# A fused four-layer graph network on one core: sums of squares by transposes and a VectorE sum, inverse degrees spread by two DMAs, incidence products earlier

## What is computed

```python
def hypergraph_conv(x, adj, W, b):
    H = (adj != 0).astype(x.dtype)
    w = adj.reshape(N, -1)[:, :C]            # first row of adj
    xw = jnp.einsum('ncd,hd->nch', x, W)
    Dn = jnp.einsum('nce,ne->nc', H, w)
    Dn = jnp.where(Dn > 0, 1.0 / Dn, 0.0)    # inverse degrees of the nodes
    Be = 1.0 / H.sum(axis=1)
    m = Be[:, :, None] * jnp.einsum('nce,nch->neh', H, xw)
    return Dn[:, :, None] * jnp.einsum('nce,neh->nch', H, m) + b
h = jax.nn.relu(hypergraph_conv(x, adj, W1, b1))      # 512 features
h = layer_norm(h, gamma, beta)                         # needs the mean of h*h
y = hypergraph_conv(h, adj, W2, b2)
```

## Time and profile before

| what | us |
|---|---|
| median of 3 runs | 1412.56 |
| lowest and highest of them | 1412.31, 1417.0 |
| span of the profiled execution | 1411.1 |
| PE busy | 1367.8 (97%) |
| DVE busy | 1271.7 (90%) |
| ACT busy | 1053.6 (75%) |
| POOL busy | 946.2 (67%) |

### The profile page before, as it was taken

How to read it: one execution, slowest core, us unless ns; L and a number is a source line. 1 busy time by engine, 2 the same in 40 slices (tenths; PEclk the granted TensorE clock), 3 DMA queues, 4 the chain that set the end, 5 groups by cost and what they waited for, 6 DMA issues and landing times.

```text
span 1411.1 us, 33599 instructions
## 1 busy us (share of the span) xinstructions
PE 1367.8 (97%) x8954; PEld 1249.5 (89%) x8954; DVE 1271.7 (90%) x5267; ACT 1053.6 (75%) x2345; POOL 946.2 (67%) x972
## 2 busy tenths in 40 slices
PE   7789999999999999999999999999999999999986
PEld 6678999999999999999999999999999999999975
DVE  6879999999999999999999999999999999999884
ACT  4557777877777887777887777787777788777764
POOL 5657766667766666766666776666786666676533
PEclk9899999999999999999999999999999999999999
DMA  4000111101111101111110111110111111111001
GB/s 127 31 31 23 39 39 54 54 23 45 52 39 50 52 29 43 47 52 37 52 47 27 45 52 37 52 52 22 45 52 45 44 52 35 39 45 37 31 31 53
DMA packets 75384, 62.16 MB, mean 44 GB/s; under 512 B 3013, under 2 KB 70985, under 8 KB 75338
## 3 DMA queue, kind: packets, MB, share of 16 engines
q1 hardware_dynamic: 75338, 61.63, 13.7%
HBM read 36.45 MB, written 16.78 MB: 38 GB/s over the span
## 4 chain that ended last, share of the span: by engine, by line
PE 92%; DVE 5%; issue 2%; ACT 1%; POOL 0%; DMA 0%; DVEq 0%; ACTq 0%; POOLq 0%
PE ps L371 39%; PE ps L356 25%; PE ps L375 20%; PE ps L477 4%; PE ps L432 3%; DVE stats L1590 1%; DVE prod L1774 1%; PE ps L633 0%; DVE h L1602 0%; DVE x L1737 0%; PE ps L629 0%; DVE x L1685 0%; DVE z L1730 0%; DMA adj_f<-in_adjT 0%; DVE el L1675 0%
## 5 line engine op out<-in xcount | busy, mean ns | idle before, releaser
L1315 POOL TENSOR_TENSOR x3n<-p,x 128x512 f32<-128x512 f32 x63 | 80.9, 1284 | 259.8 <-ACT p L982 259.8
L1275 POOL TENSOR_TENSOR hT_lo<-hT,hT_hi 128x512 fp32r<-128x512 f32 x126 | 161.3, 1302 | 57.0 <-ACT hT L924 42.1
L1255 POOL TENSOR_TENSOR rs<-var_e,neg_half 128x4 f32<-128x4 f32 x160 | 165.2, 1033 | 23.7
L903 ACT ACTIVATE p<-ps,rs 128x256 f32<-128x256 f32 (+1 forms) x256 | 136.6, 597 | 29.1 <-DVE sij L1691 28.8
L371 PE MATMUL ps<-wl_hi,h2T_hi 128*128 128x512 f32 (+1 forms) x512 | 149.1, 373 | 0.7 <-DVE x L1737 0.7
L356 PE MATMUL ps<-p,alT 128*128 128x256 f32 (+1 forms) x512 | 142.9, 382 | 0.5 <-DVE p L1715 0.5
L371 PE MATMUL ps<-wl_lo,h2T_hi 128*128 128x512 f32 (+1 forms) x512 | 132.8, 341 | 0.0
L375 PE MATMUL ps<-wl_hi,h2T_lo 128*128 128x512 f32 (+1 forms) x512 | 132.2, 340 | 0.0
L1590 DVE BATCH_NORM_STATS2 stats<-x 128x6 f32<-128x256 f32 x256 | 108.8, 425 | 5.7
L1000 ACT ACTIVATE h3T_hi<-ps 128x512 fp32r<-128x512 f32 x64 | 38.3, 598 | 91.0 <-PE ps L477 87.1
L924 ACT ACTIVATE hT_hi<-ps,cols_sb 128x512 fp32r<-128x512 f32 x128 | 87.4, 683 | 21.7 <-PE ps L375 21.5
(11 more groups left out here) (192 smaller groups left out, 4607.8 us busy)
## 6 DMA issues: line engine op xcount, KB each, us to landing
x_in<-in_x SPq DMA_DIRECT2D x32, 512.0 KB, 3.5
out_x<-x SPq DMA_DIRECT2D x32, 512.0 KB, 3.2
adj_f<-in_adjT SPq DMA_DIRECT2D x32, 256.0 KB, 2.8
adj_m<-in_adjT SPq DMA_DIRECT2D x32, 256.0 KB, 2.9
adj_l<-adj_m SPq DMA_DIRECT2D x32, 256.0 KB, 2.4
vqk<-in_l_wk SPq DMA_DIRECT2D x3, 256.0 KB, 4.6
x<-in_w1T SPq DMA_DIRECT2D x1, 512.0 KB, 6.7
x<-in_w2T SPq DMA_DIRECT2D x1, 512.0 KB, 7.7
```

Of the source, the lines that this page charges most:

```text
L903: return act.activation(dst, src, ACT.Copy, scale=scale)
L1255: pool.tensor_tensor(rs[:, layer, :], var_e[:, layer, :], neg_half[:], ALU.pow).then_inc(done, G)
L1275: pool.tensor_tensor(hTs[1][:, hc, :], hT[:, hc, :], hTs[0][:, hc, :], ALU.subtract).then_inc(S["hT_lo"], 1)
L1315: pool.tensor_tensor(x3n[:, s], p0[:, s], x2[:, s], ALU.add).then_inc(S["x3_ready"], 2)
```

## The change

It has three parts. First, `front_sums` no longer multiplies the squares with a column: it transposes each 128x128 block of `sq` into the banks `z` (columns 260 to 387), and DVE sums every row of it (`front_squares`, new, at the head of `front_variance`); the factor 1/512 moves into the last operation of the variance. Second, for all groups but the first two (`early`), the inverse degrees are spread by DMA: SP stores the column of four to a row in DRAM, waits for it, and loads that row into all 128 partitions (`spread_degrees`); `next_d` leaves PE's loop, and `next_gt` reads the SBUF tile `deg_sp` in place of the PSUM bank. Third, `next_s` moves on PE from between two `front_c2` to right behind `front_sums`, into the banks 7 and 5 in place of 3 and 4; `copy_s` on ACT and `next_degrees` on DVE move forward with it, and `copy_s` now copies the degrees too, so that DVE reads them from `s_sb`.

```diff
+        deg_row = nc.dram_tensor("deg_row", [1, G * C], F32, kind="Internal").ap()
+        deg_sp = sb("deg_sp", G, C)
+        s_sb = sb("s_sb", G, C + 1)
...
+        def early(r):
+            return not r.steady and r.i < 1
+        def s_bank(r):
+            return "s" if early(r) else "s2"
...
             def load_adj(r):
                 wait(sp, S["pen_ready"], r.front(G))
+                wait(sp, S["gt_ready"], r.front(G))
...
+            def spread_degrees(r):
+                sp.wait_ge(S["deg_ready"], r.next(G))
+                with nc.allow_non_contiguous_dma(reason="a column of four becomes a row"):
+                    sp.dma_start(deg_row.rearrange("a (g p) -> p (a g)", g=G), deg[:, 2, :]).then_inc(S["rd_stored"], 16)
+                sp.wait_ge(S["rd_stored"], r.loads(r.i - 1))
+                sp.dma_start(deg_sp[:].rearrange("p g c -> p (g c)"),
+                             deg_row.broadcast_to((P, G * C))).then_inc(S["rd_loaded"], 16)
...
             def next_s(r, b):
-                if b == 0:
-                    wait(pe, S["z_ready"], r.front(G))
+                if early(r):
+                    if b == 0:
+                        wait(pe, S["z_ready"], r.front(G))
+                elif b == 0:
+                    wait(pe, S["p2_copied"], r.mid(G))
                 elif b == 1:
-                    wait(pe, S["zb_ready"], r.mid(G))
+                    wait(pe, S["p2_copied"], r.mid(2))
...
             def late_h3(r, b):
                 if b == 0:
                     wait(pe, S["p2_copied"], r.mid(2))
+                    if r.has_next:
+                        wait(pe, S["s_copied"], r.next(G))
...
             def front_sums(r, g):
                 pe.wait_ge(S["sq_done"], r.front(G))
-                product(bank("z", g)[:, D + 2:D + 3], lambda c: sq[:, 0, g * C:(g + 1) * C],
-                        lambda c: mean_w[:, 0:1], 1).then_inc(S["hsums_ready"], 1)
+                pe.transpose(bank("z", g)[:, SQ:SQ + P], sq[:, 0, g * C:(g + 1) * C],
+                             ident[:]).then_inc(S["hsums_ready"], 1)
...
                     front_sums(r, 3)
+                if r.has_next:
+                    next_s(r, 0)
+                    next_s(r, 1)
                 if r.has_mid:
                     mid_b2(r)
...
                     mid_ap(r, 0)
-                if r.has_next:
-                    next_d(r)
...
             def degrees():
-                b = BANK["s"]
-                return (ps[:, b[0]:b[1] + 1:b[1] - b[0], 0:2 * (C + 1)]
-                        .rearrange("p b (g c) -> p b g c", g=2)[:, :, :, C])
+                return s_sb[:, :, C]
...
             def next_gt(r):
                 dve.wait_ge(S["s_copied"], r.next(G))
-                dve.wait_ge(S["rd_spread"], r.next(G))
-                dve.tensor_tensor(gt[:], bank("d").rearrange("p (g c) -> p g c", g=G), s_sb[:],
-                                  ALU.mult).then_inc(S["gt_ready"], G)
+                if early(r):
+                    dve.wait_ge(S["rd_spread"], r.next(G))
+                    rows_of = bank("d").rearrange("p (g c) -> p g c", g=G)
+                else:
+                    dve.wait_ge(S["rd_loaded"], r.loads(r.i - 1))
+                    rows_of = deg_sp[:]
+                dve.tensor_tensor(gt[:], rows_of, s_sb[:, :, 0:C], ALU.mult).then_inc(S["gt_ready"], G)
...
+            def front_squares(r):
+                dve.wait_ge(S["hsums_ready"], r.front(G))
+                dve.tensor_reduce(hsq[:], four("z")[:, :, SQ:SQ + P], AX_X, ALU.add).then_inc(S["hsq_ready"], G)
             def front_variance(r):
-                dve.wait_ge(S["hsums_ready"], r.front(G))
+                front_squares(r)
...
-                dve.tensor_tensor(hmean[:, 1, :], four("z")[:, :, D + 2], hmean[:, 0, :],
-                                  ALU.subtract).then_inc(S["hvar_ready"], G)
+                dve.wait_ge(S["hsq_ready"], r.front(G))
+                dve.scalar_tensor_tensor(hmean[:, 1, :], hsq[:], 1.0 / DH, hmean[:, 0, :], ALU.mult,
+                                         ALU.subtract).then_inc(S["hvar_ready"], G)
...
                     tail_norm(r)
+                if r.has_next:
+                    next_degrees(r)
                 if r.has_late:
                     late_low(r, 0)
```

More of the change, by code:

```diff
@@ L79, in gnn_stack @@
     K2, K1, K0, KALL = 0, D + 2, 2 * D + 2, 3 * D + 2
+    SQ = D + 4
     R = {}
@@ L146, in gnn_stack @@
         hmean = sb("hmean", 2, G)
+        hsq = sb("hsq", G)
         z = sb("z", G, D)
@@ L325, in body @@
                     load_mask(past)
+                if r.has_next:
+                    spread_degrees(r)
             def opening(r):
@@ L499, in mid_p10 @@
                     wait(pe, S["p2_copied"], r.mid(G))
+                    if r.has_next:
+                        wait(pe, S["s_copied"], r.next(2))
                 elif g == 2:
                     wait(pe, S["x1_ready"], r.front(2))
+                    if not r.steady and r.i == 1:
+                        wait(pe, S["s_copied"], r.next(G))
                     if not r.steady and r.i == GROUPS:
@@ L539, in front_sums @@
                 pe.wait_ge(S["sq_done"], r.front(G))
-                product(bank("z", g)[:, D + 2:D + 3], lambda c: sq[:, 0, g * C:(g + 1) * C],
-                        lambda c: mean_w[:, 0:1], 1).then_inc(S["hsums_ready"], 1)
+                pe.transpose(bank("z", g)[:, SQ:SQ + P], sq[:, 0, g * C:(g + 1) * C],
+                             ident[:]).then_inc(S["hsums_ready"], 1)
             def mid_ap(r, g):
                 if g == 0:
-                    if not r.steady and r.i == 1:
-                        wait(pe, S["deg_ready"], r.next(G))
+                    wait(pe, S["zb_ready"], r.mid(G))
                 elif g == 1:
@@ L695, in body @@
                     front_c2(r, 2)
-                if r.has_next:
-                    next_s(r, 0)
-                    next_s(r, 1)
-                if r.has_front:
                     front_c2(r, 3)
@@ L975, in copy_s @@
                 act.activation(s_sb[:, 2 * b:2 * b + 2, :],
-                               bank("s", b)[:, 0:2 * (C + 1)].rearrange("p (g c) -> p g c", g=2)[:, :, 0:C],
+                               bank(s_bank(r), b)[:, 0:2 * (C + 1)].rearrange("p (g c) -> p g c", g=2),
                                ACT.Copy).then_inc(S["s_copied"], 2)
@@ L1020, in centre_logits @@
             def centre_logits(r, b):
+                if b == 1:
+                    wait(act, S["p10_copied"], r.mid(1))
                 centre(1, x1, bank("hp", b).rearrange("p (g d) -> p g d", g=2), b, r.front, S["nm1_ready"], S["hp_ready"], 2 * b)
@@ L1051, in body @@
                     copy_p2(r, 3)
+                if r.has_next:
+                    copy_s(r, 0)
+                    copy_s(r, 1)
                 if r.has_late:
@@ L1640, in degrees @@
             def degrees():
-                b = BANK["s"]
-                return (ps[:, b[0]:b[1] + 1:b[1] - b[0], 0:2 * (C + 1)]
-                        .rearrange("p b (g c) -> p b g c", g=2)[:, :, :, C])
+                return s_sb[:, :, C]
             def degree_bounds(r):
                 dve.wait_ge(S["s_copied"], r.next(G))
-                dve.tensor_scalar(deg[:, 0, :].rearrange("p (b g) -> p b g", b=2), degrees(), TINY, None,
+                dve.tensor_scalar(deg[:, 0, :], degrees(), TINY, None,
                                   ALU.max).then_inc(S["deg_a"], G)
@@ L1655, in degree_masked @@
                 dve.wait_ge(S["deg_b"], r.next(G))
-                dve.scalar_tensor_tensor(deg[:, 2, :].rearrange("p (b g) -> p b g", b=2), degrees(), 0.0,
-                                         deg[:, 1, :].rearrange("p (b g) -> p b g", b=2), ALU.is_gt,
+                dve.scalar_tensor_tensor(deg[:, 2, :], degrees(), 0.0, deg[:, 1, :], ALU.is_gt,
                                          ALU.mult).then_inc(S["deg_ready"], G)
```

16 lines of the change are left out of this document (4 added, 12 removed).

## The result

| | median, us | lowest to highest | ratio to before, 95% interval |
|---|---|---|---|
| before | 1412.43 | 1412.26 to 1417.0 | |
| changed | 1596.69 | 1591.61 to 1599.96 | 1.129 [1.126, 1.132] |

A forecast was written before the change was run, and what follows sets the result against it. PE sets the round, DVE just behind: 28 rounds of 2.30 us longer give 64.4, rounds 1 and 2 2.5, rounds 0 and 31 0.5; 67.4 on 1411.1 is 1478.5, plus 1.46 about 1480 us; range 1436 to 1500.

The forecast's parts named there:

- What bounds the kernel: PE sets the 41.86 us round; DVE is less than 1 us behind, with 0.17 slack at the fourth `mid_ap`.
- The sum on DVE: New DVE sum over 512 columns, on the path to `z`: taken as 0.60 us, bounds 0.41 and 0.69.
- The spread: Store and load on SP take twice 2.9 us, hidden before `gt`; PE saves 0.44 a round without `next_d`.
- rival E: DMAs late at 7.7 us each: `gt` ends near 726, round up to 5.9 longer, 1588 us; chance 0.04.
- a wait of 2.3 us on PE: At PE's fourth `mid_ap`: a wait of about 2.3 us each steady round, released by `h3T_lo`.
- The stall at `late_h3`: PE at `late_h3` waits for the copies of `s`: about 0.25 us a round.
- `wh` late enough to lose: DVE's `wh` comes 2.88 us behind ACT's second centring and waits for POOL: about 1.3 us long.
- The threshold between 2.70 and 2.87: `wh`'s distance behind ACT's second centring: at 2.70 us it gets in ahead of POOL, at 2.87 it loses.
- `gt` loses twice: After `wh` loses, `gt` loses to POOL's second `add_x4`: 2.47 us late, round 2.30 longer; chance 0.30.
- rival A: `wh` waits, `gt` slips in before POOL's second half: round 1.05 longer, 1442 us; chance 0.27 with or without B'.
- B', the power: Third degrees operation on DVE waits for POOL's power: 0.39 later, 1492 us; chance 0.22 with two waits.

The follow-up runs named there:

- single-pass sums: Kernel before, with the sums of squares still a product with a column but in the one-pass format, nothing new on DVE: 1434.20 us, ratio 1.014.
- the wait on POOL: POOL starts its two `add_x4` only when `wh` is ready: kernel before 1409.64 us; with the one-pass column products for the squares 1403.25.
- a quick store of pieces far apart: Changed kernel, storing 512 pieces of 4 bytes 64 bytes apart in another DRAM tensor, later inverse degrees left out: 1454.28 us.
- PE kept busy over the wait: Changed kernel with 16 unread products of 128x512 added on PE ahead of its fourth `mid_ap`: 1529.80 us, ratio 1.082.
- the kernel without the DMAs: Changed kernel with parts one and three, inverse degrees spread by four PE transposes in every group as before: 1421.86 us, ratio 1.006.
- the kernel with the constant row: Changed kernel with both DMAs left out, `deg_sp` filled once with a constant, `gt` still reading two SBUF tiles: 1452.81 us, ratio 1.028.
- the first part alone: Kernel before with only the squares summed by four transposes and a sum on DVE: 1455.33 us, ratio 1.029.
- Without the DMAs: At the time 1452.81: changed kernel with both DMAs left out and `deg_sp` filled once with a constant; ratio 1.028.

## Why the prediction was wrong, step by step

**What bounds the kernel: held.** What PE saves is gained only as far as DVE can follow. The single-pass sums show it, with the wait on POOL: 0.20 a round left of 0.35, where 0.17 was worked out.

**The sum on DVE: held.** 0.69 long, 0.60 to the next, as worked out.

**The spread: the step that failed.** "DMAs of this kernel land 2.9 us after issue ... hidden." The 2.9 is the price of a DMA of 256 KB in pieces of 512 bytes; it was taken for a store of 512 single elements, of which the prediction itself says that no row shows it. It takes 8.4 to 11.2 us. The load, priced at 2.9 too, takes 3.1 behind a quick store of pieces far apart, but 5.5 behind this one, since its first packets come late; the prediction had no term for that, and what holds them back isn't shown. Both together come to 13.7 us from the store's issue in the round shown (13.5 to 15.2 over all), close to the upper bound of twice 7.7 that was written down as rival E and given a chance of 0.04. The bound was there; the choice of the nearer row was wrong, since the row differed in the one thing that mattered, the shape of the pieces.

**The clock: missing.** No term of the sum had it, though it had a wait of 2.3 us on PE. Some 1.5 to 1.8 us a round were lost to the lower clock, and without them E's 1588 would have been too high: with PE kept busy over the wait the time is 1529.80. That E came within 9 us of the result is luck in part.

**The stall at `late_h3`: right place, wrong size.** 0.25 by the sum; 0.29 idle in the kernel without the DMAs, but 0.47 from start to start.

**`wh` late enough to lose: not here.** In the kernel with the constant row `wh` comes 2.81 us after the centring, not 2.88, and gets in 0.06 ahead of POOL (695.84 and 695.90 above). The threshold between 2.70 and 2.87 was right; the first part alone reached 2.87 and lost.

**`gt` loses twice: wrong; once.** Without the DMAs the time is 1452.81, against 1442 by the sum of rival A, which also has one wait; what the 11 us between them are made of was not worked out. In the changed kernel itself the term never came up: the DMAs moved `gt` to 719.68, to the end of POOL's row.

**B', the power: wrong.** The third operation of the degrees takes 0.16 at 705.66, while POOL's power runs:

```profile
705.20 1.04 POOL L1283 TENSOR_TENSOR rs<-var_e,neg_half 128x4 f32<-128x4 f32 x1
```

It is so in every steady round. Early in the run the same operation does wait, there for the end of a row of POOL operations on 512 columns (46.63 + 0.67 = 47.30 against 43.82 + 3.46 = 47.28):

```profile
46.63 0.67 DVE L1682 SCALAR_TENSOR_TENSOR deg<-s_sb,deg 128x4 f32<-128x4 f32 x1
43.82 3.46 POOL L1378 TENSOR_TENSOR wl_lo<-vqk,wl_hi 128x512 fp32r<-128x512 f32 x3
```

The Trainium skill, "SBUF — State Buffer", section "Who interferes with whom", says that a DVE instruction with two SBUF inputs contends with a GpSimd instruction that reads SBUF, that the port pair they share is an exclusive lock, and that issue order, not the shape, decides who blocks. Where POOL works on 512 columns the traces agree (`wh` 1.31, `gt` 1.75, this operation 0.67); on the power of four elements they do not (0.16 inside 1.04), and the measurement decides.

## What to carry to other kernels

Price a DMA by a row with pieces of the same size and the same neighbourhood, and where there is none, take the pessimistic bound as the forecast when the transfer has a consumer on the critical path; a store of a column of floats into one row of DRAM is the case to avoid. A wait on a TensorE that never waited can cost more than its length: here some 1.5 us a round beside a wait of about 4, since the granted clock fell to 0.50 behind it. And where VectorE and GpSimd hold each other up, a tenth of a microsecond decided here who waits for whom: let the one with idle time behind it wait on purpose.

## What the runs showed of the hardware

The packets of the slow store are all recorded between 706 and 707.5 us. From there to 717.0 none is: not until SP goes on at 714.44, and not in the 2.6 us behind it, though the load is issued by then (DMA view of the two stretches):

```profile
DMA packets 528, 0.00 MB, mean 1 GB/s; under 512 B 528, under 2 KB 528, under 8 KB 528
```
```profile
DMA packets 0, 0.00 MB, mean 0 GB/s; under 512 B 0, under 2 KB 0, under 8 KB 0
```

So the engines had handed the elements over by then, and 7 us went by until the store counted as done. The store with its pieces 64 bytes apart also has 528 packets, at the same distance from its issue (0.9 to 1.3 us), and is done half a microsecond behind the last one. The whole difference lies behind the last packet, and it outlasts the store: the first packet of the load comes 10.7 to 12.5 us behind the slow store's issue, whether SP could issue the load after 8.4 us or only after 11.2. The Trainium skill, "DMA: Bandwidth & Descriptors", section "Anatomy of one DMA — SWDGE (gpsimd) path", puts most of a DMA's fixed cost of about 2 us into the receipt of the write, longest where the target is HBM; it says so of DMAs that GpSimd issues, and these are SP's. The trace agrees with it in kind: the time lies behind the last packet. Its size is another: 8.1 us side by side against 1.8 apart, for as many bytes.
